# A mixer's input projections: one float32 product each, or three float32r products of high and low halves

## The reference

```python
zxbcdt = x_norm @ in_proj_w.T                    # 256 -> 1160 columns
z, xBC, dt = jnp.split(zxbcdt, [512, 512 + 640], axis=-1)
xBC = silu(causal_conv4(xBC) + conv_b)           # 512 features x, 64 B, 64 C
dt = softplus(dt + dt_bias)                      # 8 step sizes a token
# a scan over the tokens with exp(dt * A), B, C gives y
yg = rmsnorm(y * silu(z)) * gnorm_w              # z: the gates
out = p_fast * x_norm + p_mamba * (yg @ out_proj_w.T)
```

## Time and profile before

| | us |
|---|---|
| median of 3 runs | 974.23 (972.43 to 978.69) |
| the profiled execution: its time | 975.07 |
| its span | 973.2 |
| TensorE busy | 879.9 |
| VectorE busy | 668.0 |
| ScalarE busy | 500.5 |
| GpSimd busy | 335.8 |

### The profile page before, as it was taken

How to read it: one execution, slowest core, us unless ns; L and a number is a source line. 1 busy time by engine, 2 the same in 40 slices (tenths; PEclk the granted TensorE clock), 3 DMA queues, 4 the chain that set the end, 5 groups by cost and what they waited for, 6 DMA issues and landing times. The chain is left out here.

```text
span 973.2 us, 13403 instructions
## 1 busy us (share of the span) xinstructions
PE 879.9 (90%) x4318; PEld 483.7 (50%) x4318; DVE 668.0 (69%) x1373; ACT 500.5 (51%) x996; POOL 335.8 (35%) x344
## 2 busy tenths in 40 slices
PE   5889898999999999499989999998989999959996
PEld 2445554333333325266657888787433322624575
DVE  4875677888889944345558776875699897545653
ACT  3796444677777784012126565563207777333321
POOL 7326636300000001146567666563420000126823
PEclk9999998999999999699989999999998999959998
DMA  5040028123213920853240000000200550075200
GB/s 159 1 148 14 1 39 115 19 52 51 48 41 56 285 77 1 287 211 120 98 120 1 1 1 1 1 1 1 82 3 17 200 197 1 1 274 190 66 18 27
DMA packets 41512, 73.65 MB, mean 76 GB/s; under 512 B 8948, under 2 KB 27636, under 8 KB 40292
## 3 DMA queue, kind: packets, MB, share of 16 engines
q1 hardware_dynamic: 36228, 59.51, 21.3%
q0 software_dynamic: 4400, 13.11, 4.1%
q10 hardware_dynamic: 816, 0.17, 0.1%
HBM read 49.51 MB, written 10.49 MB: 62 GB/s over the span
## 5 line engine op out<-in xcount | busy, mean ns | idle before, releaser
L1086 DVE TENSOR_REDUCE c_amx<-PS 128x1 f32<-128x512 f32 x256 | 159.1, 683 | 27.4 <-PE PS L985 27.1
L1179 ACT ACTIVATE c_aE<-PS 128x512 f32<-128x512 f32 x256 | 132.6, 602 | 47.1 <-PE PS L997 46.9
L1917 POOL TENSOR_SCALAR s_Pn<-s_Pr,s_rs 128x512 f32<-128x512 f32 x64 | 100.2, 1567 | 56.3 <-DVE s_rs L1959 56.2
L72 POOL TENSOR_SCALAR rstd<-mv 128x4 f32<-128x4 f32 (+1 forms) x10 | 2.4, 243 | 332.5 <-DVE mv L96 332.4
L985 PE MATMUL PS<-c_aKs,c_aQs 99*128 99x512 bf16 x256 | 96.1, 386 | 5.4 <-DMA c_aQs<-area 3.9
L997 PE MATMUL PS<-c_aQs,c_aKs 99*128 99x512 bf16 x256 | 94.5, 380 | 3.5 <-ACT c_aE L1179 2.3
L1086 DVE TENSOR_REDUCE h_amx<-PS 128x1 f32<-128x512 f32 x128 | 79.6, 683 | 8.6 <-PE PS L985 8.3
L1179 ACT ACTIVATE h_aE<-PS 128x512 f32<-128x512 f32 x128 | 67.6, 600 | 21.6 <-PE PS L997 21.3
L2055 ACT ACTIVATE s_Pr<-PS,s_nmx 128x512 f32<-128x512 f32 x64 | 44.2, 690 | 65.4 <-DVE s_nmx L1952 65.4
L1008 PE MATMUL PS<-c_aE,c_VB 128*17 128x512 f32 x512 | 67.4, 598 | 0.1
L985 PEld LDWEIGHTS PS<-c_aKs,c_aQs 99*128 99x128 bf16 x256 | 24.9, 97 | 79.4 <-DVE c_amx L1086 55.5
(11 more groups left out here) (491 smaller groups left out, 1958.5 us busy)
## 6 DMA issues: line engine op xcount, KB each, us to landing
area<-in_e_w SPq DMA_DIRECT2D x16, 512.0 KB, 10.0
area<-in_g_w SPq DMA_DIRECT2D x8, 1024.0 KB, 6.2
c_aKs<-area SPq DMA_DIRECT2D x48, 128.0 KB
g_B<-in_g_b SPq DMA_DIRECT2D x1, 4096.0 KB, 14.3
c_aQs<-area SPq DMA_DIRECT2D x48, 64.0 KB
h_aQs<-h_QP SPq DMA_DIRECT2D x48, 64.0 KB
early<-in_ctxT SPq DMA_DIRECT2D x2, 1024.0 KB, 7.6
e_B<-in_e_b SPq DMA_DIRECT2D x1, 2048.0 KB
```

Source lines behind the costliest of these rows:

```text
L1086: dve.tensor_reduce(self.mx[:, qt, j, half:half + 1], PS[:, n % MB, :], AX.X, ALU.max).then_inc(self.max_done, 1)
L1179: act.activation(self.E[kt % 2][:, j, :], PS[:, MB + x % XB, :], ACT.Exp, scale=0.25).then_inc(self.exp_done, 1)
L1917: pool.tensor_scalar(Pn[g % NPB][:, :], Pr[g % NPB][:, :], rs[:, g % NPB:g % NPB + 1], None, ALU.mult).then_inc(pn_ready, 1)
```

## The change

Every projection is computed as three matmuls of type float32r on halves. The high half of a value is its rounding to float32r, the low half is the value less its high half (also float32r). The products are high x high, high weight x low input, low weight x high input, all added in PSUM.

VectorE makes the high halves: of the weights in two instructions, `FIRST` (1296 numbers a partition: features, B, C, step sizes) and `LAST` (1024: the gates), and of `XT` in four, one a quarter. It also makes the four low quarters of `XT`, which are written over `XT`. GpSimd makes the low halves of the weights in two instructions, ahead of its work on `base`; they are written over `w_in`. The high halves use memory that the scan needs only later. For `inputs` and the step sizes TensorE goes through the parts outermost, both batches in each, and asks for both banks of the ring before the first matmul. The shift of `EARLY` by 8 words is an alignment.

```diff
         @block.gpsimd
             pool.tensor_tensor(sc[:, 0, :], sc[:, 0, :], mhalf[:, :], ALU.pow).then_inc(dev_ready, 1)
+            for n, cols in enumerate((FIRST, LAST)):
+                pool.wait_ge(wh_ready, n + 1)
+                pool.tensor_tensor(w_low[:, :, cols], w_in[:, :, cols], w_high[:, :, cols].bitcast(F32),
+                                   ALU.subtract).then_inc(wl_ready, 1)
             pool.wait_ge(dev_ready, 1)
         @block.vector
+            def high_weights(cols):
+                dve.tensor_copy(w_high[:, :, cols], w_in[:, :, cols]).then_inc(wh_ready, 1)
+            dve.wait_ge(w_in_in, 16)
+            high_weights(FIRST)
+            for g in range(KD * B):
+                b, k = divmod(g, KD)
+                dve.wait_ge(xT_ready, g + 1)
+                dve.tensor_copy(x_high[g][:, :], XT[:, k, b * S:(b + 1) * S]).then_inc(xh_ready, 1)
+            high_weights(LAST)
+            for g in range(KD * B):
+                b, k = divmod(g, KD)
+                dve.wait_ge(xh_ready, g + 1)
+                dve.tensor_tensor(x_low[:, k, b * S:(b + 1) * S], XT[:, k, b * S:(b + 1) * S], x_high[g][:, :].bitcast(F32),
+                                  ALU.subtract).then_inc(xl_ready, 1)
             dve.wait_ge(sh.const_in, 16)
             dve.tensor_copy(identb[:, :], ident[:, :])
         @block.tensor
+            PARTS3 = ((0, 0), (0, 1), (1, 0))
+            WEIGHTS = (w_high, w_low)
+            def split_ready(w_part, x_part, g, n):
+                pe.wait_ge((wh_ready, wl_ready)[w_part], n)
+                pe.wait_ge((xh_ready, xl_ready)[x_part], g)
+            def projected(dst, cols):
+                for w_part, x_part in PARTS3:
+                    for b in range(B):
+                        split_ready(w_part, x_part, KD * (b + 1), 1)
+                        for k in range(KD):
+                            last = pe.matmul(dst[b], WEIGHTS[w_part][:, k, cols], inputs_part(x_part, k, b),
...
+                        if (w_part, x_part) == PARTS3[-1]:
+                            yield last
             def inputs(n):
                 _, col, _ = convs[n]
-                for b in range(B):
-                    bank = ring(2 * n + b)
-                    for k in range(KD):
-                        last = pe.matmul(bank, w_in[:, k, col:col + P], XT[:, k, b * S:(b + 1) * S],
-                                         start=(k == 0), stop=(k == KD - 1))
+                dst = [ring(2 * n + b) for b in range(B)]
+                for last in projected(dst, slice(col, col + P)):
                     last.then_inc(proj_done, 1)
             def gates(i):
...
+                for w_part, x_part in PARTS3:
+                    split_ready(w_part, x_part, KD * B, 2)
+                    for k in range(KD):
+                        last = pe.matmul(bank, inputs_part(x_part, k, b)[:, t * P:(t + 1) * P],
+                                         WEIGHTS[w_part][:, k, Z0:Z0 + DI],
```

More of the change, by code:

```diff
@@ L21 @@
 AREA = 16384
-EARLY = 8488
+EARLY = 8496
 KD = D // P
@@ L211, in mamba_stage @@
     DT0, B0, X0, Z0 = 2 * DI + 2 * DS, 2 * DI, DI, 0
+    IN = DT0 + HEADS
+    FIRST, LAST = slice(X0, IN), slice(Z0, X0)
     PARTS = 3
@@ L229, in mamba_stage @@
     CV = [early.take([P, B, S]) for n in range(2)]
-    w_in = early.take([P, KD, 2 * DI + 2 * DS + HEADS])
+    early.take([P, 4])
+    w_in_at = sh.early_at + 4 * early.used
+    w_in = early.take([P, KD, IN])
     keys = sh.keys
@@ L260, in mamba_stage @@
     Btok, GT = sb("Btok", [P, NT, DS]), sb("GT", [P, NT, P])
+    chunk_at = nc.sbuf_base
     XHt, XD, XDs, XHD, T1, YG, YGT = (
         [sb(f"{name}{n}", [P, DI]) for n in range(2)] for name in ("XHt", "XD", "XDs", "XHD", "T1", "YG", "YGT"))
+    w_high = nc.alloc_sbuf_tensor_at("m_w_high", [P, KD, IN], F32R, offset=sh.area_at + 4 * area.used)
+    w_low = nc.alloc_sbuf_tensor_at("m_w_low", [P, KD, IN], F32R, offset=w_in_at)
+    x_high = [nc.alloc_sbuf_tensor_at(f"m_x_high{g}", [P, S], F32R, offset=chunk_at + (2 * 5 + g) * 4 * DI)
+              for g in range(KD * B)]
+    x_low = nc.alloc_sbuf_tensor_at("m_x_low", [P, KD, T], F32R, offset=sh.xt_at)
     E, W = ([area.take([P, HEADS, P]) for n in range(2)] for name in "EW")
@@ L292, in mamba_stage @@
     x_sum = sem("x_sum")
+    wh_ready, wl_ready, xh_ready, xl_ready = (sem(n) for n in ("wh_ready", "wl_ready", "xh_ready", "xl_ready"))
     def states_before(n):
@@ L747, in ring, with inputs_part @@
                 return PS[:, 4 + j % 4, :]
+            PARTS3 = ((0, 0), (0, 1), (1, 0))
+            WEIGHTS = (w_high, w_low)
+            def inputs_part(part, k, b):
+                g = KD * b + k
+                return x_high[g][:, :] if part == 0 else x_low[:, k, b * S:(b + 1) * S]
+            def split_ready(w_part, x_part, g, n):
[7 more added lines that the diff above has]
+                            last = pe.matmul(dst[b], WEIGHTS[w_part][:, k, cols], inputs_part(x_part, k, b),
+                                             start=((w_part, x_part) == PARTS3[0] and k == 0),
+                                             stop=((w_part, x_part) == PARTS3[-1] and k == KD - 1),
+                                             skip_group_check=True)
+                        if (w_part, x_part) == PARTS3[-1]:
+                            yield last
             def inputs(n):
                 _, col, _ = convs[n]
-                for b in range(B):
-                    bank = ring(2 * n + b)
-                    for k in range(KD):
-                        last = pe.matmul(bank, w_in[:, k, col:col + P], XT[:, k, b * S:(b + 1) * S],
-                                         start=(k == 0), stop=(k == KD - 1))
+                dst = [ring(2 * n + b) for b in range(B)]
+                for last in projected(dst, slice(col, col + P)):
                     last.then_inc(proj_done, 1)
@@ L759, in gates @@
                 bank = ring(2 * len(convs) + i)
-                for k in range(KD):
-                    last = pe.matmul(bank, XT[:, k, i * P:(i + 1) * P], w_in[:, k, Z0:Z0 + DI],
-                                     start=(k == 0), stop=(k == KD - 1))
+                b, t = divmod(i, TB)
+                for w_part, x_part in PARTS3:
[3 more added lines that the diff above has]
+                                         WEIGHTS[w_part][:, k, Z0:Z0 + DI],
+                                         start=((w_part, x_part) == PARTS3[0] and k == 0),
+                                         stop=((w_part, x_part) == PARTS3[-1] and k == KD - 1))
                 last.then_inc(proj_done, 1)
             inputs(0)
[L766 to L769, removed]
+            for last in projected([PS[0:HEADS, 2 + b, :] for b in range(B)], slice(DT0, DT0 + HEADS)):
                 last.then_inc(dt_mm, 1)
@@ L1370, in __init__ @@
         self.wq, self.wk, self.wv = (early.take([P, KD, D]) for _ in range(3))
-        early.used = 2 * (B * (3 + S) + B * S) + KD * 1160
+        early.used = 2 * (B * (3 + S) + B * S) + 4 + KD * 1160
         self.mask = early.take([P, B, self.NK])
@@ L3464, in decoder @@
         sh.X, sh.XN = (sh.XX[:, h * NT * D:(h + 1) * NT * D].rearrange("p (t c) -> p t c", t=NT) for h in range(2))
+        sh.xt_at = nc.sbuf_base
         sh.XT = ctx.enter_context(nc.sbuf_tensor("XT", [P, KD, T], F32))
@@ L3489, in decoder @@
         sh.early_held = ctx.enter_context(ExitStack())
+        sh.early_at = nc.sbuf_base
         sh.early = sh.early_held.enter_context(nc.sbuf_tensor("early", [P, EARLY], F32))
```

## The result

| | us |
|---|---|
| median after, 8 runs | 980.96 (978.21 to 987.99) |
| median before beside it, 8 runs | 975.02 (972.43 to 978.69) |
| ratio | 1.0068, 95% interval 1.004 to 1.0096 |
| profiled execution after: time, span | 978.21, 976.4 |

What follows compares the result with a forecast made beforehand. ScalarE and VectorE were taken to bound the first 62 us behind inputs(1), TensorE only up to it. Late halves +4.8 and saved gate waits -0.2 gave 4.6, from 974.2 to 978.8 us; range 973.5 to 983.

Steps and rivals of the forecast that it cites:

- The split casts and the turns: Before inputs(0): VectorE's casts and two-input work alternate with GpSimd's subtractions, so the last low quarter ends at 22.4 us.
- TensorE's lateness at inputs(1): End of inputs(1): TensorE finishes at 32.25 us instead of 28.05, 4.2 late; with ScalarE's 0.6 more, +4.8.
- The term at the last gate: Last gate of the projections: taken about 4.6 us later than 61.6, from 4.8 - 0.2.
- No gain behind inputs(1): inputs(2) to gates(7): TensorE's savings lie beside VectorE and ScalarE, paying only 0.2 us in the last stretch.
- the term of -0.2: Last stretch, 54 to 62 us: cheaper matmuls save only ScalarE's waits for gates, 0.2 us.
- The move of the stall into convolve(1): VectorE's 4.4 us stall under GpSimd's tensor_tensor for `base` moves from convolve(0) to convolve(1), costing nothing.
- the cover: Ahead of convolve(2): VectorE free at 40.9, take(2) ending at 43.8, so 2.9 us of ScalarE's sequence hide the stall.
- the scan and all stages behind it are shifted as a whole.: Behind the projections: scan and later stages keep their lengths and only start later, the sum staying 4.6 us.
- a rival for the clock: Idle gaps leave TensorE at 1.2 GHz in inputs(1) and the last gates: about +5 on top, 984; chance 0.08.
- Every GpSimd instruction holds the pair: tensor_scalar too blocks VectorE's two-input work, delaying low quarters and convolve(0): +9.3, 983.5 us; chance 0.09.
- my reading, that both go on with a small loss: Beside `base`, GpSimd's tensor_scalar lets VectorE's two-input work through with a loss: 0.8 us each for x_low 2 and 3.

Runs made afterwards that it cites:

- the second measurement: The changed kernel timed again with nothing altered: 984.1 us beside 977.2 before, ratio 1.0085.
- e3_nolow: The changed kernel without GpSimd's two subtractions, TensorE using the weights' high half twice: 984.6 us beside 974.9 before, ratio 1.0035.
- e4_one: The changed kernel with only high x high for every projection, issued once all halves are there: 978.5 us beside 974.9 before, ratio 1.002.
- e5_acthigh: The changed kernel with ScalarE writing x_high from PSUM, VectorE making low halves from PSUM and casting weights before: 981.1 us beside 974.8, ratio 1.005.
- e2_delay: The kernel before, all float32, with TensorE's second batch of inputs(0) waiting for 7 unused VectorE reductions: 980.1 us beside 974.9, ratio 1.0048.
- e8_actfill: The kernel of e5_acthigh plus 12 and 7 spare matmuls on TensorE: 974.4 us beside 977.2 before, ratio 0.9984.

## Why the prediction was right, and where it wasn't

The direction and the mechanism at the front of the kernel held; the time lies in the range (973.5 to 983). That it does so is in part luck: 1.35 us too much at the front stood against 2.3 to 3.8 us of the scan that the sum had not at all, and the second measurement, 984.1 beside 977.2, would not have lain in the range as a time. One thing was put down as a rival that belongs in the sum.

- **The split casts and the turns**: right. FIRST ended at 11.9 as worked out, GpSimd's first subtraction at 15.04 (15.3), its second at 19.41 (20.1), x_low at 21.15 (22.4). The last was over-sized by 1.2: LAST was cast 0.4 earlier, x_low 2 and 3 followed at 0.6 each beside `base`, not 0.8, and the rest was won at x_low 0 and 1 and the second subtraction. e3_nolow shows the cause, GpSimd's turns.
- **TensorE's lateness at inputs(1)**: 4.2 forecast, 2.9 measured (31.2 against 28.3), by that 1.2 and step sizes of 3.65 instead of 4.0, less 0.3 that the six matmuls before them took longer. take(1) ended 3.5 late (33.04), not 4.8. The term at the last gate was 3.25, not 4.6.
- **No gain behind inputs(1)**: right, shown by e4_one, where two thirds of the matmuls there were missing and it bought nothing. convolve(2) was 3.52 late and the last gate 3.25, so the term of -0.2 was -0.27; silu(4) follows 14.8 us behind the start of convolve(2), as before.
- **The move of the stall into convolve(1)**: right in place, but the cover was worked out wrongly. `base` took 12.84 us for its eight instructions, not 10.9. Four lasted 1.22; the one beside x_low 2 and 3 and the casts behind them lasted 2.70, and the three beside convolve(0) 2.31, 1.51 and 1.52. VectorE was free at 42.3, 0.2 us before take(2) ended, and not 2.9; half of that difference is VectorE 1.4 later than forecast, half ScalarE 1.3 sooner.
- **The step that failed: "the scan and all stages behind it are shifted as a whole."** They are not. TensorE fell to half clock in the scan in both traces of the changed kernel, which cost 3.8 and 2.3 us. I had a rival for the clock at 0.08 and placed it at inputs(1) and the last gates, where nothing was lost; its price, about 5 us, was near, its place and its chance were wrong. I took as evidence against it that the old kernel kept its clock over gaps of 1.6 us. That says little: the old kernel had 13.6 of 15 us busy in this stretch, while the changed one has 4.0 us idle before 41.59 and ran at half clock from 42.7 to 46.1 (which cost nothing at the last gate); and in the scan the same idle time of 1.9 us went with full clock in the one and half clock in the other.
- **Every GpSimd instruction holds the pair** (the exceptionless reading of the Trainium skill, page "SBUF — State Buffer", section "Who interferes with whom"): fell in its price, as VectorE never waited for a tensor_scalar. x_low 2 and 3 took 0.68 each beside `base`, convolve(0)'s three 1.29, 1.46 and 1.47. But my reading, that both go on with a small loss, was too mild for GpSimd: its instruction that had begun 0.07 us behind the first of convolve(0) took 1.1 us longer than alone, as if held for most of it, and only the later ones ran side by side at 1.5. For tensor_tensor the page's full block is what the trace shows, 3.08 and 2.73 us. Its statement that a VectorE instruction with at most one SBUF input, outside the 2-port perf modes, does not contend agrees with e5_acthigh for the low halves: 0.74 us each beside a running subtraction. The tensor_scalar behind them has one SBUF input too and was held to 2.65; whether it ran in such a mode no run here shows.

What stays open: why the clock falls at 66 in one kernel and at 127 in another, and not at all in the scan of the kernel before, which has the same idle time there. The runs show that filling the idle stretches moves or removes the falls; e2_delay shows that the moment matters too. The loss behind 400 us differs from execution to execution and was not attributed: e8_actfill ended its scan 1.6 us ahead of before and its span 2.0 behind it.

## What to carry to other kernels

Cutting an engine's work only helps where its end is what the next engine waits for; find that stretch first, and count what the cheaper form needs before it can start. A GpSimd tensor_tensor and VectorE's casts and two-input instructions count there as the work of one engine. Make such halves where one input is in PSUM, or on ScalarE. And when TensorE gets less to do between waits, look at the granted clock of the stage behind it: matmuls that compute nothing, put into its idle time, were here worth 3 to 7 us in the changed kernel and 1 to 2 in the kernel before, so give them to both kernels before comparing.

## What the hardware showed that I had not expected

- A TensorE with fewer products ran at 1.2 GHz for 65 us on end (e4_one), and the untouched stage behind paid 6.6 us.
- One kernel's executions spread with the clock: before, with 0.966 or 0.967 of full as the mean, mostly took 971 to 975 us, with 0.950 to 0.956 mostly 978 to 981.
- An addition of 64 numbers a partition lasted 4.28 us behind a GpSimd tensor_tensor of 128x2048 (0.23 before): here the stall ended with GpSimd's instruction, whatever the size of VectorE's.
- GpSimd's tensor_scalar of 128x256 took 1.22 us beside an idle VectorE (1.24 on average in the earlier trace rows), 1.5 beside convolve(0)'s second and third instruction, and 2.3 where it had begun just behind the first.
